# Attention's layer norm by a product with (identity - mean), squares read from PSUM, and projection weights centred once

## The reference, cut to what matters

```python
def _ln_c(v, eps=1e-06):
    m = jnp.mean(v, axis=1, keepdims=True)
    s = jnp.var(v, axis=1, keepdims=True)
    return (v - m) / jnp.sqrt(s + eps)

def _L0_conv_ref(x, qkv_w, proj_w, proj_b, bias_table):
    x = jnp.roll(x, (-SHIFT, -SHIFT), axis=(2, 3))
    qkv = jnp.einsum('bchw,oc->bohw', x, qkv_w)
    ...  # windows of 8 x 8 pixels, 4 heads of 16 channels
    attn = jnp.einsum('wnqd,wnkd->wnqk', q, k) * SCALE
    ...  # + bias by relative position, + shift mask
    attn = jax.nn.softmax(attn, axis=-1).reshape(B * nW, NH, N, N)
    ...  # times v, back to the image, projection with bias, roll back

x = x + _L0_conv_ref(_ln_c(x), L0_conv_qkv_w, L0_conv_proj_w, L0_conv_proj_b, L0_conv_bias_table)
```

## Time and profile before

| | us |
|---|---|
| time, median of 3 runs (lowest, highest) | 6351.58 (6346.39, 6352.13) |
| profiled execution, first to last instruction | 6346.6 |
| PE busy over the span | 5083.0 (80%) |
| DVE busy | 4318.6 (68%) |
| ACT busy | 3662.3 (58%) |
| POOL busy | 1158.8 (18%) |

### The profile page before, as it was taken

How to read it: one execution, slowest core, us unless ns; L and a number is a source line. 1 busy time by engine, 2 the same in 40 slices (tenths; PEclk the granted TensorE clock), 3 DMA queues, 4 the chain that set the end, 5 groups by cost and what they waited for, 6 DMA issues and landing times. The chain is left out here.

```text
span 6346.6 us, 131027 instructions
## 1 busy us (share of the span) xinstructions
PE 5083.0 (80%) x47166; PEld 3296.2 (52%) x47166; DVE 4318.6 (68%) x9746; ACT 3662.3 (58%) x6942; POOL 1158.8 (18%) x1068
## 2 busy tenths in 40 slices
PE   7887886538968885799969997407999999948887
PEld 4664664224533332599969995104555555523332
DVE  7896897884359897622223446697777777758896
ACT  5675775555547774522243224456767676746774
POOL 2332332053200002400000000131211111121110
PEclk9998998858989997699989999758999999979999
DMA  1111112333348885200000124237666666537777
GB/s 33 38 32 32 35 38 74 79 94 85 107 146 277 281 284 169 79 0 0 0 0 0 57 102 128 70 98 99 81 83 83 82 83 81 68 115 244 249 245 225
DMA packets 794230, 646.32 MB, mean 102 GB/s; under 512 B 496551, under 2 KB 644199, under 8 KB 793779
## 3 DMA queue, kind: packets, MB, share of 16 engines
q1 hardware_dynamic: 792755, 639.06, 40.6%
q0 software_dynamic: 1024, 1.05, 0.1%
HBM read 549.78 MB, written 90.20 MB: 101 GB/s over the span
## 5 line engine op out<-in xcount | busy, mean ns | idle before, releaser
L2357 PE MATMUL sw_pC<-sw_row,sw_wc 128*128 128x128 f32 x10160 | 1158.9, 274 | 56.2 <-DVE sw_row L2232 54.9
L2357 PEld LDWEIGHTS sw_pC<-sw_row,sw_wc 128*128 128x128 f32 x10160 | 1147.7, 191 | 58.2 <-DVE sw_row L2232 55.5
L2791 PE MATMUL sp_pC<-sp_work,sp_bands 64*64 64x512 f32 (+11 forms) x14592 | 985.5, 428 | 43.4 <-issue 43.4
L2220 DVE SCALAR_TENSOR_TENSOR sw_row<-sw_pC,sw_y 128x128 f32<-128x128 f32 x1016 | 337.5, 332 | 792.1 <-PE sw_pC L2357 792.1
L2791 PEld LDWEIGHTS sp_pC<-sp_work,sp_bands 64*64 64x64 f32 x14592 | 600.3, 133 | 431.8 <-issue 363.8
L2730 ACT ACTIVATE sp_pC<-sp_pC,sp_par 128x512 f32<-128x512 f32 x832 | 598.4, 741 | 369.9 <-PE sp_pC L2791 346.7
L1771 DVE TENSOR_TENSOR t_z<-t_z,t_ht 128x1024 f32<-128x1024 f32 x512 | 630.1, 1273 | 72.9 <-DMA t_z<-gate_rows 71.5
L2289 ACT ACTIVATE sw_y<-sw_row 128x128 f32 (+1 forms) x762 | 265.3, 348 | 592.8 <-DVE sw_row L2220 592.8
L1934 PE MATMUL t_pO<-t_z,t_ew 128*64 128x512 f32 x2048 | 521.0, 626 | 107.4 <-DVE t_z L1771 104.2
L2687 DVE TENSOR_TENSOR sp_work<-sp_work,sp_pC 128x512 f32<-128x512 f32 x512 | 350.9, 687 | 169.1 <-ACT sp_pC L2730 168.6
L307 POOL TENSOR_TENSOR wa_sc<-wa_sc,wa_sm 128x1024 f32<-128x1024 f32 x128 | 243.6, 1903 | 679.4 <-DVE wa_sm L396 679.4
(11 more groups left out here) (380 smaller groups left out, 9823.1 us busy)
## 6 DMA issues: line engine op xcount, KB each, us to landing
t_z<-gate_rows SPq DMA_DIRECT2D x512, 512.0 KB, 8.5
sp_bands<-windows SPq DMA_DIRECT2D x128, 512.0 KB
c_spent<-tokens SPq DMA_DIRECT2D x128, 256.0 KB, 2.7
cb_xs<-tokens SPq DMA_DIRECT2D x128, 256.0 KB, 2.9
wa_xs<-in_x SPq DMA_DIRECT2D x64, 256.0 KB, 3.0
tokens<-wa_xt SPq DMA_DIRECT2D x128, 128.0 KB, 1.9
tokens<-cb_h SPq DMA_DIRECT2D x64, 256.0 KB, 3.0
t_xs<-tokens SPq DMA_DIRECT2D x32, 512.0 KB, 11.3
```

The source lines that it names most:

```text
L2220: dve.scalar_tensor_tensor(row[par][c][:, :, PAD:PAD + P2], pC[c][:, 0:2 * P2].rearrange("p (b w) -> p b w", b=2), 0.0, line(sweep, c, i), ...
L2357: ins = pe.matmul(pC[c][:, 0:2 * P2], wc[:, sweep, m, :], row[1 - par][c][:, :, m:m + P2], start=(m == 0), stop=(m == 4))
L2791: ins = pe.matmul(out[halves[to], :, low * lo:low * hi], band[halves[k], (NV * g + j) % BANDS, q, AT[k][tap], :], v[halves[k], :, low * at ...
```

## The change

A matrix `center_w` = identity - `mean_w` is built by GpSimd. The product that gave the mean now gives x - mean itself in PSUM. There is no `xc` and no DVE centring any more; ScalarE squares straight from PSUM, and this frees `pL` for the next product. The write of `h` multiplies the uncentred `xs` with the root, and to make up for it the three projection weights are centred once at the start by a product with `center_w` (since (W (I - M)) x = W ((I - M) x)). In ScalarE's order the first square moves ahead of `save_probs` in step j=0, and the second one to the top of step j=1.

```diff
--- before.py
+++ after.py
@@ -122,8 +122,10 @@
         a = Arena(nc, ctx, "wa")
         ident = a.sb("ident", [128, 128])
         mean_w = a.sb("mean_w", [128, 128])
+        center_w = a.sb("center_w", [128, 128])
         w_rows = a.sb("w_rows", [128, 4, 128])
         w_cols = a.sb("w_cols", [128, 4, 128])
+        w_raw = a.sb("w_raw", [128, 3, 128])
         pb = a.sb("pb", [128, 1])
         eps = a.sb("eps", [128, 1])
         iota_q = a.sb("iota_q", [128, 1], mybir.dt.int32)
...
@@ -215,12 +217,12 @@
                     strip(bp, i, bp * STRIPS + i, i % NX, False, i == STRIPS - 1)
                 end(bp, bp * STRIPS + STRIPS)
 
-        def normalised(eng, par):
+        def normalised(eng, par, k):
 
             for w0, w1, c0, c1, col in ((0, 15, 0, WS, SHIFT), (15, 16, 0, 4, W - 4), (15, 16, 4, 8, 0)):
                 def part(t):
                     return t[:, :, col:col + (w1 - w0) * (c1 - c0)].rearrange("p r (w c) -> p w r c", c=c1 - c0)
-                ins = eng.tensor_tensor(h[:, par, w0:w1, :, c0:c1], part(xc), part(sq), ALU.mult)
+                ins = eng.tensor_tensor(h[:, par, w0:w1, :, c0:c1], part(xs[:, k, :, :]), part(sq), ALU.mult)
             return ins
 
         def steps(n, k, first, last, body):
@@ -297,6 +299,7 @@
             for g in range(2):
                 link(pool.memset(mean_w[64 * g:64 * g + 64, 64 * g:64 * g + 64], 1.0 / C))
             eye(pool, link, ident[:, :])
+            link(pool.tensor_tensor(center_w[:, :], ident[:, :], mean_w[:, :], ALU.subtract))
             link(pool.iota(iota_q[:, :], pattern=[[0, 1]], base=0, channel_multiplier=1))
             pool.iota(iota_k[:, :], pattern=[[1, 64]], base=0, channel_multiplier=0).then_inc(const_ready, 1)
 
@@ -395,37 +398,24 @@
                 dve.wait_ge(row_sums, u + 1)
                 dve.reciprocal(sm[:, j % 2, 1, :, :], sm[:, j % 2, 0, :, :]).then_inc(sum_ready, 1)
 
-            def center(m, half, k):
-                rows = slice(4 * half, 4 * half + 4)
-                dve.wait_ge(mean_ready, 2 * m + half + 1)
-                dve.wait_ge(h_ready, m + 1)
-                dve.tensor_tensor(xc[:, rows, :], xs[:, k, rows, :],
-                                  pL[:, :].rearrange("p (r c) -> p r c", c=W), ALU.subtract).then_inc(centered, 1)
-
-            def write_h(m, par, done):
+            def write_h(m, par, done, k):
                 dve.wait_ge(rstd_ready, m + 1)
                 dve.wait_ge(qkv_ready, 2 * done + 2)
-                normalised(dve, par).then_inc(h_ready, 1)
+                normalised(dve, par, k).then_inc(h_ready, 1)
 
             def begin(bp, n):
-                for half in range(2):
-                    center(n, half, 0)
-                write_h(n, 0, NSTEP * n)
+                write_h(n, 0, NSTEP * n, 0)
                 save_v(NSTEP * n, 0)
 
             def strip(bp, i, n, k, first, last):
                 def body(s, j, after, back1, back2):
                     if back1:
                         softmax_sum(*back1[0:2])
-                    if j == 1 and not last:
-                        center(n + 1, 1, (k + 1) % NX)
                     softmax_shift(s, j, last)
                     if after:
                         save_v(*after[0:2])
                     if j == 2 and not last:
-                        write_h(n + 1, (k + 1) % 2, NSTEP * n)
-                    if j == 0 and not last:
-                        center(n + 1, 0, (k + 1) % NX)
+                        write_h(n + 1, (k + 1) % 2, NSTEP * n, (k + 1) % NX)
                 steps(n, k, first, last, body)
 
             def end(bp, n):
@@ -436,7 +426,10 @@
         @block.scalar
         def _(act):
             act.wait_ge(w_turned, 1)
-            act.activation(w_cols[:, :, :].rearrange("p m c -> p (m c)"), pL[:, :], ACT.Copy).then_inc(w_ready, 1)
+            act.activation(w_cols[:, 3, :], pL[:, 384:512], ACT.Copy)
+            act.activation(w_raw[:, :, :].rearrange("p m c -> p (m c)"), pL[:, 0:384], ACT.Copy).then_inc(w_saved, 1)
+            act.wait_ge(w_centered, 1)
+            act.activation(w_cols[:, 0:3, :].rearrange("p m c -> p (m c)"), pL[:, 0:384], ACT.Copy).then_inc(w_ready, 1)
 
             def save_qk(s, j):
                 act.wait_ge(qkv_ready, 2 * s + 4)
@@ -471,8 +464,9 @@
 
             def square(m, half):
                 rows = slice(4 * half, 4 * half + 4)
-                act.wait_ge(centered, 2 * m + half + 1)
-                act.activation(sq[:, rows, :], xc[:, rows, :], ACT.Square).then_inc(squared, 1)
+                act.wait_ge(mean_ready, 2 * m + half + 1)
+                act.wait_ge(h_ready, m + 1)
+                act.activation(sq[:, rows, :].rearrange("p r c -> p (r c)"), pL[:, :], ACT.Square).then_inc(squared, 1)
 
             def log(m, half):
                 rows = slice(4 * half, 4 * half + 4)
@@ -503,6 +497,8 @@
                 def body(s, j, after, back1, back2):
                     if j == 3 and not first:
                         save_turned(n - 1, (k - 1) % 2, 0)
+                    if j == 1 and not last:
+                        square(n + 1, 1)
                     if after:
                         save_qk(*after[0:2])
                     if back2:
@@ -510,15 +506,13 @@
                     if j == 2 and not last:
                         log(n + 1, 1)
                         root(n + 1)
-                    if j == 1 and not last:
-                        square(n + 1, 1)
                     exponential(s, j)
+                    if j == 0 and not last:
+                        square(n + 1, 0)
                     if back1:
                         save_probs(back1[0])
                     if back2:
                         save_proj(*back2)
-                    if j == 0 and not last:
-                        square(n + 1, 0)
                     if j == 1 and not last:
                         log(n + 1, 0)
                     if j == 3 and not first:
@@ -544,6 +538,9 @@
             for m in range(4):
                 ins = pe.transpose(pL[:, 128 * m:128 * m + 128], w_rows[:, m, :], ident[:, :])
             ins.then_inc(w_turned, 1)
+            pe.wait_ge(w_saved, 1)
+            pe.matmul(pL[:, 0:384], center_w[:, :], w_raw[:, :, :].rearrange("p m c -> p (m c)"), start=True,
+                      stop=True).then_inc(w_centered, 1)
             pe.wait_ge(w_ready, 1)
 
             def qkv(s, j, par, n=None):
@@ -600,14 +597,13 @@
             def mean(m, half, k):
                 pe.wait_ge(x_in[k], 8 * (m - k) + 32)
                 if half == 1:
-                    pe.wait_ge(centered, 2 * m + 1)
-                pe.matmul(pL[:, :], mean_w[:, :], xs[:, k, 4 * half:4 * half + 4, :], start=True,
+                    pe.wait_ge(squared, 2 * m + 1)
+                pe.matmul(pL[:, :], center_w[:, :], xs[:, k, 4 * half:4 * half + 4, :], start=True,
                           stop=True).then_inc(mean_ready, 1)
 
             def variance(m, half):
-                pe.wait_ge(squared, 2 * m + half + 1)
                 if half == 0:
-                    pe.wait_ge(centered, 2 * m + 2)
+                    pe.wait_ge(squared, 2 * m + 2)
                 else:
                     pe.wait_ge(log_ready, 2 * m + 1)
                 pe.matmul(pL[:, :], mean_w[:, :], sq[:, 4 * half:4 * half + 4, :], start=True,
```

More of the change, by code:

```diff
@@ L140, in stage_window_attention @@
         xs = a.sb("xs", [128, NX, 8, 128])
-        xc = a.sb("xc", [128, 8, 128])
         sq = a.sb("sq", [128, 8, 128])
@@ L166, in stage_window_attention @@
         w_turned = a.sem("w_turned")
+        w_saved = a.sem("w_saved")
+        w_centered = a.sem("w_centered")
         w_ready = a.sem("w_ready")
@@ L169, in stage_window_attention @@
         mean_ready = a.sem("mean_ready")
-        centered = a.sem("centered")
         squared = a.sem("squared")
```

## The result

The changed kernel takes 6366.09 us (median of 8 runs, 6356.16 to 6371.69), the kernel before 6351.85 us; the ratio is 1.0021, 95% interval 1.0012 to 1.0030: 14 us slower, at the edge of what is called no change (0.2%). One of the eight runs of the kernel before took 7839.6 us, in a slower state of the chip, and the ratio leaves it out. The forecast was 6361 us, with a range of 6349 to 6374 us around it. The changed kernel's profiled execution spans 6354.3 us against 6346.6, and took 6356.16 us, the shortest of its runs.

What follows compares the result with a forecast made beforehand. The strip was taken as bound by TensorE's queue behind the second mean product, not by DVE. Clean strips 4.8, jumps 2.0, first strips 1.1 and start 1.7 sum to 9.6 us on 6351.6: 6361 us, range 6349 to 6374.

Steps and rivals of the forecast that it cites:

- Where the strip is closed: Attention strip: closed by mean product, TensorE's queue, variance product, root and write of h, with DVE off it; 29.61 us.
- The 64 centrings are worth 0: DVE's centring subtractions, 43.6 us in sum, lie in time in which DVE would wait; removing them gains 0.
- The square takes 0.60 and the product slips 0.43: Step j=0: first square from PSUM takes 0.60 us; second mean product, waiting for it, starts 0.43 us later.
- Slack of 0.18 to 0.25, 0.20 per clean strip: Behind the values product, slack absorbs part of the slip; each of 24 clean strips costs 0.20 us more, 4.8 us.
- The start, 1.7 us: Kernel start: centring the projection weights delays the first mean product from 18.51 to 20.2 us, 1.7 us later.
- The first strips, 1.1: First strips of the two passes: second mean product starts later, 0.4 us and 0.7 for the very first; 1.1 us together.
- The jumps, 2.0: Four strips behind a jump back in the loop: product 0.6 us later, some 0.1 absorbed; 0.5 each, 2.0 us.
- the clock: Rival: longer TensorE idle before the second mean product halves its clock in each strip, +43 us, 6404 us; chance 0.04.
- Half clock inside clean strips: Sign of being wrong: TensorE at half clock (1.2 instead of 2.4 GHz) in strips not behind a jump or first.
- The other signs: Strips 29.8 us, product 1.6 us behind exponential, L613 not waiting for logarithm, first product near 20.2 us, DVE busy near 25.5.
- the forecast's 9.6: Whole kernel: 4.8 clean strips, 2.0 jumps, 1.1 first strips, 1.7 start; 9.6 us slower in sum.
- the terms named for a change slower by more than 12.7 us: Whole kernel: clock rival, two thirds of the no-slack case (6368 us, 0.18), a seventh of the main forecast (0.55); stated 0.27.

Runs made afterwards that it cites:

- the new wait alone: Kernel before, centrings kept, second mean product made to wait for the first square, right behind the exponential of j=0: 6380.92 us, ratio 1.0046.
- both moves that take TensorE's queue from behind it: Changed kernel, separately: first square ahead of the exponential of j=0, 6308.03 us; second mean product behind the scores of j=1, 6317.14 us.
- DVE's work back: Changed kernel with two unused half-strip sums per strip added on DVE where the centrings stood: 6365.38 us, ratio 1.0024.
- one call moved: Changed kernel with the first square of the next strip moved ahead of the exponential of j=0 on ScalarE: 6308.03 us, ratio 0.9927.
- the run with the work given back: Changed kernel with the first square ahead of the exponential of j=0, plus two unused DVE sums where the centrings stood: 6318.17 us, ratio 0.9948.
- only its scores moved: Kernel before with the second mean product placed behind the scores of j=1 in TensorE's order: 6327.55 us, ratio 0.9959.

## Why the prediction held, and where it was off

By its own steps. *Where the strip is closed*: shown, by the new wait alone (slip 0.65, strip 0.66) and by both moves that take TensorE's queue from behind it. *The 64 centrings are worth 0*: shown by giving 39.1 of the 43.6 us back. *The square takes 0.60 and the product slips 0.43*: 0.59 and 1.60 - 1.22 = 0.38. *Slack of 0.18 to 0.25, 0.20 per clean strip*: 0.16; the 0.59 us between L588 and L609 is TensorE's own pace, as forecast, and the slip shrinks from 0.37 to 0.13 us between these two products, so the slack was 0.24; from there 0.15 arrive at h, and the strip is 0.16 longer. *The start, 1.7 us*: 20.31 - 18.51 = 1.80; the first product of before waited there for the image's DMA and not, as its description says, for the copy, which had ended 0.7 us earlier. *The first strips, 1.1*: wrong in sign for the first pass. In spite of the 1.80 us its first residual add starts at 86.98 us against 87.09, while TensorE's clock rose earlier (scores of 1.10 us at 40.80, where the kernel before still had 1.98 at 39.34). *The jumps, 2.0*: 1.07, the four of them together 130.33 against 129.26 us; in the other two profiles of the changed kernel they take 131.66 and 132.15, 2.4 and 2.9 more than before, so the first figure is chance.

The step that was wrong is the clock, which the sum has at nothing. I gave it 0.04 as a case of all strips or none, because TensorE had kept its clock after 2.20 us of idle time at another place. That row was a single case: at the same place of the second pass, in the same profile of before, the same idle time was followed by a fall:

```profile
584.65 1.90 PE L554 MATMUL wa_pQK<-wa_h,wa_w_cols 128*128 128x256 f32 x4 [2.21 <-DVE wa_h L223]
```

And in the changed kernel's three profiles the projection at 63 us, again behind 2.2 us of idle time, took 1.49, 1.44 and 2.08 us instead of 1.13. In the strips the clock came as a case of some: 9 of 66 behind 1.74 us of idle time, 3 of 22 behind 1.75 with DVE's work back, 10 of 22 behind 2.03, none of 22 behind the 1.37 of before, none of 44 behind 0.71. Half clock inside clean strips was one of the prediction's own signs of being wrong, and it came. The other signs came out as forecast: strips of 29.77 us, the product 1.60 us behind the exponential, no wait for the logarithm at L609, the first product at 20.31, DVE busy 25.7 us (25.5 forecast).

At 1.6 us each and 3 per execution the falls are some 5 us, and with them the forecast's 9.6 would have been 14.5, where 14.2 were measured. That this fits is in part luck. At the last residual add the three profiles stand 9.6 to 12.6 us behind before; without their slow strips it is 5 to 8 us, less than the 9.6 forecast for the stage. In the first profile the 9.6 us are 3.5 from the 22 clean distances, 3.3 from the two falls, 1.1 from the jumps and 1.8 from the turn of the passes, with nothing left of the start. And the rest of their spans, where nothing was changed, is 5347.1, 5351.5 and 5355.2 us against 5349.0, so single executions differ there by 8 us, over half of the whole effect. The chances were also out by a little: the terms named for a change slower by more than 12.7 us, which is where 14.2 lies, add up to 0.24 and not to 0.27.

The page of the Trainium skill on the clock gate (TensorE: Matmul & The Clock Gate, Loop structure matters more than you think), which I had set aside because the wait seemed too short, was the nearer one in kind, though its bad case is a long wait for a DMA: a wait between products did cost clock. The advice of the Trainium skill to work on the engine of highest occupancy (Perfetto Trace Analysis, Identifying the Most-Contended Engine) would have given 6310 us; the changed kernel did not get there, yet with one call moved it took 6308 us. DVE was the engine to relieve, but only once the waits let it be the bound: of the 45 us by which that kernel beats before, 10 are what the lighter DVE brings, by the run with the work given back; the rest is the order of work, and the kernel before with only its scores moved, centrings and all, already took 6327.55.

Open: in which strips the clock falls (three profiles of one kernel agree in few places), how many fall in the executions without a profile, and whether the square ahead of the exponential alone, in the kernel before, would have gained as much; there the square needs DVE's centring, and no run tried it.

## What to carry to other kernels

Work taken off the busiest engine is worth what the engine would not have waited anyway; read that at the instruction behind it, by what releases it. When the new consumer of a shared PSUM bank sits on another engine, look at what stands in TensorE's queue behind the next product into that bank, and put the consumer into a gap of its engine ahead of the long instruction (here 0.59 us of work into 1.19 us of waiting) instead of behind it. A wait that grows by 0.4 us can also cost clock.

## What the runs showed of the hardware

TensorE's clock after a short idle time is a matter of chance in part: at the same place in each strip of a program, 1.74 us of idle time was followed by half clock in 9 of 66 strips, and 2.03 us, in another program, in 10 of 22; 2.20 us ahead of a projection left full speed at 63 us of the kernel before and half clock at 585 us; and the same 2.9 us at a loop's jump left it high in one execution and at half in another. A fall slowed the scores and the projections of one step and cost 1.6 us. With the 1.74 us cut to 0.71 by added products, none of 44 strips fell. A square of 128x512 fp32 took 590 ns from PSUM and 627 from SBUF.
